# Attention 1 of a four-layer kernel with its scores computed turned: the probabilities come out transposed, the maxima ride along as two rows of the operand

## Reference

```python
q = Wq @ x + bq                       # 256 x 256 by 256 x 1024, for each batch b of 8
k, v = (Wk @ ctx + bk) @ proj_k, (Wv @ ctx + bv) @ proj_v      # 256 x 64, computed earlier
q, k, v = (t.reshape(b, HD, H, -1) for t in (q, k, v))         # HD = 16, H = 16 heads
scores = jnp.einsum('bdhn,bdhk->bhnk', q, k) / HD ** 0.5       # 1024 queries x 64 keys a head
prob = jax.nn.softmax(scores, axis=-1)
out = Wm @ einsum('bhnk,bdhk->bdhn', prob, v) + bm
x = x + tanh(gate) * out              # x is normalised before it; after it come its row statistics
```

## Time and profile before

| | us |
|---|---|
| three runs, median | 1507.66 (1507.24 to 1511.41) |
| the profiled execution | 1511.91 |
| its span, first to last instruction | 1510.2 |
| attention 1 in it | 1085 to 1425 |
| busy over the span: PE / DVE / ACT / POOL | 1381.5 / 974.5 / 747.1 / 427.6 |

### The profile page before, as it was taken

The page is one execution under the profiler, slowest core; times in us unless marked ns, Lnnn a source line. Parts: engine busy times, 40 slices in busy tenths (PEclk is TensorE's granted clock), DMA queues, the critical chain, the costliest instruction groups (busy, mean ns, idle before and its releaser), DMA issues. The chain is left out here.

```text
span 1510.2 us, 28515 instructions
## 1 busy us (share of the span) xinstructions
PE 1381.5 (91%) x10774; PEld 1123.1 (74%) x10782; DVE 974.5 (65%) x1564; ACT 747.1 (49%) x1881; POOL 427.6 (28%) x473
## 2 busy tenths in 40 slices
PE   6998799999999999987999999979779999999388
PEld 6997788979889898855888888868556666666244
DVE  4363277767767767664233256648657999998487
ACT  4231167766767767762111111013157777777286
POOL 0010001101011010111011113223468888887224
PEclk9999889999999999999999999989899999999789
DMA  6743454552544526555534551102332222221023
GB/s 224 240 154 93 81 134 116 141 138 71 147 116 127 151 71 176 140 168 184 186 130 172 195 223 57 42 24 74 109 101 64 64 64 63 63 63 43 1 84 140
DMA packets 127910, 174.93 MB, mean 116 GB/s; under 512 B 27799, under 2 KB 96919, under 8 KB 127792
## 3 DMA queue, kind: packets, MB, share of 16 engines
q1 hardware_dynamic: 127792, 173.26, 39.4%
HBM read 86.94 MB, written 35.29 MB: 81 GB/s over the span
## 5 line engine op out<-in xcount | busy, mean ns | idle before, releaser
L1148 ACT ACTIVATE a_prob<-a_psS,a_negmax 128x256 f32<-128x256 f32 x512 | 237.2, 484 | 159.2 <-DVE a_negmax L1063 159.2
L1063 DVE TENSOR_REDUCE a_negmax<-a_psS 128x4 f32<-128x1024 f32 x128 | 154.1, 1204 | 68.5 <-PE a_psS L956 66.8
L881 POOL COPY a_recip<-a_recip_head 128x256 f32<-128x256 f32 x64 | 25.7, 402 | 528.6 <-DVE a_recip_head L1113 528.6
L931 PE MATMUL a_psQ<-a_xT_hi,wide 128*128 128x256 f32 x912 | 171.1, 288 | 0.4
L1366 PE MATMUL m_psY<-w_ffn,m_a_hi 128*128 128x512 f32 x512 | 160.3, 395 | 9.3 <-DVE m_a_lo L1422 9.3
L1366 PE MATMUL m_psY<-wide,m_a_hi 128*128 128x512 f32 x512 | 159.3, 392 | 6.8 <-DVE m_a_lo L1414 6.8
L966 PE MATMUL a_psT<-ident,a_prob 128*128 128x128 f32 x1024 | 138.6, 280 | 14.3 <-ACT a_probT L1165 5.8
L931 PEld LDWEIGHTS a_psQ<-a_xT_hi,wide 128*128 128x128 f32 x912 | 138.8, 189 | 9.1 <-issue 6.0
L966 PEld LDWEIGHTS a_psT<-ident,a_prob 128*128 128x128 f32 x1024 | 117.4, 144 | 23.6 <-issue 12.6
L1165 ACT COPY a_probT<-a_psT 128x512 f32<-128x512 f32 x208 | 116.0, 610 | 37.6 <-PE a_psT L966 36.5
L931 PE MATMUL a_psQ<-a_xT_lo,wide 128*128 128x256 f32 x456 | 127.5, 280 | 0.0
(11 more groups left out here) (233 smaller groups left out, 3017.7 us busy)
## 6 DMA issues: line engine op xcount, KB each, us to landing
a_q_stack<-a_q_hi SPq DMA_DIRECT2D x128, 128.0 KB, 2.6
a_q_stack<-a_q_lo SPq DMA_DIRECT2D x128, 128.0 KB, 2.6
c_raw<-lay_ctxT SPq DMA_DIRECT2D x16, 512.0 KB, 4.8
rows<-in_x SPq DMA_DIRECT2D x8, 1024.0 KB, 6.6
scratch_o<-a_oT SPq DMA_DIRECT2D x16, 512.0 KB, 3.0
m_x<-in_x SPq DMA_DIRECT2D x8, 1024.0 KB, 5.9
scratch_x<-m_x SPq DMA_DIRECT2D x8, 1024.0 KB, 5.1
b_q_stack<-b_q_hi SPq DMA_DIRECT2D x64, 128.0 KB, 2.3
```

Of the source, the lines that this page charges most:

```text
L881: nc.gpsimd.tensor_copy(recip[:, t % 2], recip_head[:, t % 2].unsqueeze(3).broadcast_to([P, TT, JH0, HD0])).then_inc(recip_ready, 1)
L931: last = nc.tensor.matmul(bank[:, 0:S], w[:, kt, t * P:(t + 1) * P], a[:, kt, :], start=(kt == 0 and w is wq.hi and a is xT_hi), stop=(kt ...
L1063: nc.vector.tensor_reduce(negmax[:, n % 2, :], psS[:, bank:bank + 2, :].rearrange("p a (j k) -> p (a j) k", k=S), AX_X, ALU.max, negate=Tr ...
L1148: last = nc.scalar.activation(prob[:, n % 2, j, :], psS[:, 2 * (n % 2) + j // 2, (j % 2) * S:(j % 2 + 1) * S], ACT.Exp, bias=negmax[:, n % ...
```

## The change

The unit becomes a tile of 128 channels (`t`, eight heads as four pairs `j`) by 512 queries (`h`), four a batch. The work is a list of steps `(b, k)`, k from 0 to 3 and b from -1 to 8, and each engine's program follows it.

- `scores` now makes only approximate scores (high parts alone, one bank `psS` of 128 queries x 8 heads x 64 keys) so that DVE can take negated maxima (`negmax`). It waits for the maximum before it, since there is one bank.
- `turn_shift` transposes the maxima of half a batch, ACT copies them (`copy_shift`), and `stack_shift` puts them by DMA into rows 96 and 97 of `q_stack`.
- `turned_scores` takes keys (`kT`, 98 rows: high, high and low parts, and two rows of ones) as the stationary operand and `q_stack` as the moving one. Its product is the exact score minus the maximum, keys in the partitions. ACT takes the exponential straight into `probT`. Nothing is transposed.
- `values` makes the products with V for 512 queries, and then the sums, with 0/1 matrices (`sum_of`) into `psM`. DVE takes reciprocals of 128 x 256, split into high and low parts, and `spread_reciprocals` spreads them by matmuls with a 0/1 matrix.
- `stack_query` needs three parts (high, low, high) for each of four pairs of heads: 12 DMAs of 32 rows a tile. `load_rows` repeats the keys three times (6 DMAs), and `load_keys`, `load_v1` take one DMA each; `stack_shift` takes 4 DMAs, twice a batch.
- Wq, Wm and the tables are laid out by the host. The ffn weight is loaded at the start of `ffn1_stage`.

```diff
-                for g in range(2):
-                    rows = slice(g * HALF_P, (g + 1) * HALF_P)
-                    for src, half in ((q_hi, g), (q_lo, 1 - g)):
-                        sp.dma_start(plain(q_stack)[half * HALF_P:(half + 1) * HALF_P, t, g, cols],
-                                     plain(src)[rows, m % 2, :]).then_inc(q_stacked[m], 16)
+                if a:
+                    sp.wait_ge(psP_full, 4 * TILES * (a - 1) + PJ * (k + 1))
+                sp.wait_ge(q_lo_ready, TILES * a + k + 1)
+                for part, src in enumerate((q_hi, q_lo, q_hi)):
+                    for j in range(PJ):
+                        sp.dma_start(plain(q_stack)[part * 2 * HD1:(part + 1) * 2 * HD1, t * PJ + j, cols],
+                                     plain(src)[j * 2 * HD1:(j + 1) * 2 * HD1, k % 2, :]).then_inc(q_stacked[k], 16)
+            def stack_shift(a, h):
+                if a:
+                    sp.wait_ge(psP_full, 4 * TILES * (a - 1) + 2 * PJ * (h + 1))
+                sp.wait_ge(shift_ready, 2 * a + h + 1)
+                for t in range(CT1):
+                    for e in range(2):
+                        lo = t * HT1 + e * PJ
+                        sp.dma_start(plain(q_stack)[STACKED + e:STACKED + e + 1, t * PJ:(t + 1) * PJ, h * HALF_N:(h + 1) * HALF_N],
+                                     plain(shift)[lo:lo + PJ, h, :]).then_inc(shift_stacked[h], 16)
 ...
+            for b, k in STEPS:                                   # SP
+                if k == 0 and real(b + 1):
+                    load_rows(b + 1)
+                    load_v1(b + 1)
+                if k == 1 and real(b + 2):
+                    load_keys(b + 2)
+                sa, sk = scored_tile(b, k)                       # (b + 1, k - 1) if k else (b, 3)
+                if real(sa):
+                    stack_query(sa, sk)
+                if k == 1 and real(b):
+                    stack_shift(b, 1)
+                if k == 3 and real(b + 1):
+                    stack_shift(b + 1, 0)
 ...
+            def scores(a, k, i):                                 # PE, four to a tile
+                if n:
+                    pe.wait_ge(max_ready, n)
+                nc.tensor.matmul(psS[:, :], q_hi[:, k % 2, i * P:(i + 1) * P], kbd[:, a % 2, t, :, :].rearrange("p h k -> p (h k)"),
+                                 start=True, stop=True).then_inc(scores_full, 1)
+            def turned_scores(b, k, j):                          # PE, four to a tile
+                if j == 0:
+                    pe.wait_ge(q_stacked[k], QDMAS * (b + 1))
+                    pe.wait_ge(shift_stacked[h], 64 * (b + 1))
+                if n >= 2:
+                    pe.wait_ge(exp_done, n - 1)
+                nc.tensor.matmul(psP[:, n % 2, :], kT[0:ROWS, b % 2, t * PJ + j, :, :].rearrange("p e k -> p (e k)"),
+                                 q_stack[0:ROWS, t * PJ + j, h * HALF_N:(h + 1) * HALF_N], start=True, stop=True
+                                 ).then_inc(psP_full, 1)
```

More of the change, by code:

```diff
@@ L1613, in attn1_stage, with tile_of, output_of @@
     ident = sh.ident
[L1614 to L1632, removed]
+    PAIRS1, STACKED, TILES = NH1 // 2, 3 * 2 * HD1, 4
+    ROWS = STACKED + 2
+    PJ = PAIRS1 // CT1
+    PARTS = 3
+    QDMAS = 16 * PARTS * PJ
+    def tile_of(k):
+        return k % CT1, k // CT1
+    def output_of(b, k):
+        return (b, 0, 0) if k == 3 else (b - 1, *((1, 0), (0, 1), (1, 1))[k])
     with ExitStack() as es:
@@ L1661, in attn1_stage @@
[L1661 to L1667, removed]
+        q_stack = sb("q_stack", [P, PAIRS1, D], F32R)
+        keys = sb("keys", [P, CT1, NK1])
+        kbd = sb("kbd", [P, 2, CT1, HT1, NK1], F32R)
+        krep = sb("krep", [P, PAIRS1, NK1])
@@ L1685, in attn1_stage @@
[L1685 to L1692, removed]
@@ L1697, in _, with real, scored_tile @@
+        block = es.enter_context(nc.Block())
+        STEPS = [(b, k) for b in range(-1, B + 1) for k in range(TILES)]
+        def real(b):
+            return 0 <= b < B
+        def scored_tile(b, k):
+            return (b + 1, k - 1) if k else (b, TILES - 1)
         @block.sync
         def _(sp):
[L1699 to L1703, removed]
-                    for g in range(2):
[L1705 to L1709, removed]
@@ new lines, in spread_reciprocals @@
+            def spread_reciprocals(b, h, t):
+                n = 2 * b + h
+                if t == 0:
+                    pe.wait_ge(recip_low, n + 1)
+                    pe.wait_ge(shift_ready, min(n + 2, 2 * B))
+                else:
+                    pe.wait_ge(o_ready, 2 * n + 1)
+                for part in range(2):
+                    nc.tensor.matmul(psB[:, part * S:(part + 1) * S], spread[:, t, part, :], recip_hi[:, :], start=True, stop=False)
+                    last = nc.tensor.matmul(psB[:, part * S:(part + 1) * S], spread[:, t, part, :], recip_lo[:, :],
+                                            start=False, stop=True)
+                last.then_inc(psB_full, 1)
@@ new lines, in output @@
+            def output(n, b, t, h, dt):
+                if dt == 0:
+                    if n == 0:
+                        pe.wait_ge(wm_loaded, 16)
+                    else:
+                        pe.wait_ge(y_ready, n)
+                    pe.wait_ge(o_ready, 4 * b + 2 * h + 2)
+                last = nc.tensor.matmul(psY[:, :], wmT[:, dt, t * P:(t + 1) * P], o[:, dt, h * HALF_N:(h + 1) * HALF_N],
+                                        start=(dt == 0), stop=(dt == CT1 - 1))
+                if dt == CT1 - 1:
+                    last.then_inc(out_full, 1)
```

759 lines of the change are left out of this document (368 added, 391 removed).

## The result

The changed kernel takes 1547.29 us in the median of 4 executions (1544.73 to 1553.73), the kernel before 1507.52 us (4 executions). The ratio is 1.0264, 95% interval 1.0229 to 1.0300: 39.8 us slower, where 47.4 were forecast (1555 us, range 1510 to 1582). Attention 1, from its first DMA to the end of its last row maximum, grew from 339.9 us (1084.85 to 1424.72, for the end) to 373.0 us (1084.94 to 1457.96). Another 3.7 us lie at the head of the last stage.

A forecast was written before the change was run, and what follows sets the result against it. TensorE bound the kernel before, DVE right behind; afterwards SP's DMA issuing was to bound attention 1. A later start, batches of 42.4 us and a longer end gave +47.4 us: 1555 us, range 1510 to 1582.

The forecast's parts named there:

- SP sets the batch: Attention 1: SP issues 64 DMAs a batch at 0.64 us, 41.0 us, more than PE's 37.8; main case, chance 0.52.
- T = 42.4: Length of an attention 1 batch: 19.4 us to step (b+1, 0), then 36 DMAs, 23.0 us, to step (b+1, 2).
- The wait and the half clock in T: PE idles 3 to 5 us before step (b, 2), then starts at half clock; without the clock's part T is 41.
- First turned score 1126.6: Attention 1, step (0, 0): first stack DMA at 1098, then 41 DMAs (26.2 us) and landing.
- the sum: Attention 1 from start through batches to last row maximum at 1472.1 against 1424.7: +47.4 us.
- The weight load costs nothing under 14 us: Last stage's head: ffn weight needs 8.6 us, first transposes came 14 us after the stage began, so moving it is free.
- PE's terms: TensorE in attention 1: value records and sum records run in waves of four, 1.0 us each, 2.0 together.
- The worse rival: Value records overlap in pairs only, or issues cost more: batch 45 to 48.6 us, 1573 to 1597 us; chance 0.13.
- DVE's terms: DVE in attention 1: reciprocal 2.1 us (lower bound 0.5), low parts 0.4, in all 30 us a batch.
- The first rival: DVE and PE in lockstep, SP not the bound (issue 0.50): 37.8 us a batch, 1528 us; chance 0.22.
- The faster rival: PE sets the pace, issue 0.50 or less, reciprocal near 0.5: 1496 us, needing batches under 35.3 us; chance 0.13.

The follow-up runs named there:

- e2: Changed kernel plus four more DMAs a batch on SP, into a tile nobody reads: 1567.42 us, ratio 1.0386.
- e11: e9 with the x3 work in steps 1 and 3 and the last stage's weight loaded behind GpSimd's reduction: 1509.95 us, ratio 1.0024.
- e5: Changed kernel with 4 of each query tile's 12 DMAs left out from the second batch on: 1534.78 us, ratio 1.0198.
- e7: Changed kernel with query tiles sent through DRAM, five larger DMAs a tile in place of twelve: 1525.77 us, ratio 1.0109.
- e9: e7 with DVE making the low keys behind its x3 work in step k = 1, not ahead of it: 1515.70 us, ratio 1.0054.
- e12: e11 with no early wait for the spreading table, first maxima sent before the third query tile, weight loaded in the last full batch: 1506.65 us, ratio 1.0002.
- e1: Changed kernel with the maxima's 8 DMAs a batch issued by ACT instead of SP: 1545.02 us, ratio 1.0246.
- e13: e12 with GpSimd instead of DVE normalising x2 and making the reciprocals' low parts: 1509.55 us, ratio 1.0026.

## Why the prediction was right, and by which steps

- *SP sets the batch, 41.0 us by 64 issues of 0.64.* Right, and shown by e2. The query tiles cost 0.63 and the maxima 0.65, as taken from the earlier trace rows. The keys' rows cost 0.47, the figure that the earlier trace rows had for 32 rows from DRAM and that the prediction used only as a bound; for v and the keys it was 0.43 and 0.58.
- *T = 42.4.* The term that was mis-sized. From step (0, 0), 1124.54, to step (7, 0), 1410.87, it is 40.9 a batch. The half from step (b, 2) to (b+1, 0) was forecast as 19.4; it is 19.06 in the batch shown (1270.74 to 1289.80) and 18.9 in the mean of seven. The other half, 36 DMAs, was forecast as 23.0 and is 22.0, by the cheaper DRAM reads (8 of the 36). Seven batches make 10.5 us of the error.
- *The wait and the half clock in T.* Right in part. The 28 issues between the maxima of the two halves need 17.8 us by themselves, and two of the seven halves took just that; the others took 19.0 to 19.8, so waits do come on top. PE's seven waits before step (b, 2) were 5.31, 3.89, 3.27, 2.31, 3.19, 2.81 and 1.91 us. Behind the first three and the sixth the granted clock fell to half for 3 to 7 us, and those four halves took 19.4 us in the mean, the forecast; behind the other three it stayed full, and they took 18.2. So the clock's part was there in four batches of seven, and the prediction had it in all. That it lengthened those halves is read from seven cases and not tested.
- *First turned score 1126.6, step (7, 2) 13 to 14 us behind (7, 0), the end 34.4 us later.* Measured 1124.54, 13.6 us (1410.87 to 1424.48), and 33.5 us (to 1457.96). In all the stage grew by 33.1 us where the sum had 47.4. That the ratio's 39.8 us lies nearer is luck in part: 3.7 us are the weight load, which the sum did not have, and about 4 us are the spread of executions, since the profiled one of before was a slow one.
- *The weight load costs nothing under 14 us.* Wrong, 3.7 us. The load itself took about 8.7 us, but it stretched the time before GpSimd's reduction from 5.9 to 9.5 us (e11). The prediction asked when the weight was needed, and not what its transfer delays. The Trainium skill ("GPSIMD Engine Reference", section "Instruction dispatch") says that the first call of a freshly loaded GpSimd kernel pays about 6 us for loading its code; the 5.88 and 5.84 us here agree. That the time before the reduction is code being loaded, and that this is what the 2 MB transfer slowed, is inferred from the page and e11's edit, not seen.
- *PE's terms.* Values and sums cost 34.1 + 33.5 = 67.6 us for 32 tiles, 2.1 a tile: waves of four, 2.0 forecast. The worse rival falls with it, and with issues of 0.63 and maxima of 0.65 each, not 0.76 and 0.85.
- *DVE's terms.* The reciprocal takes 1.75 us (2.1 forecast, within 0.5 to 2.1). The low part takes 1.07 on average (0.4 forecast). The sum, 30 us a batch, was right (29.5 and 31.7).
- *The first rival, lockstep at 37.8 us a batch.* This is the step that failed, unseen while SP was in front: e5 and e7 measure 40 us. Its sum of work was right and its order was not read: `low_keys` stands in DVE's list where it waits 3.3 us for ACT, and 2.0 us of x3 work lies behind it. With that put right (e9) the batch is 37.7, the 37.8 of the prediction. That it agrees so closely is chance, since e11 has 36.6 with the same work in yet another order. That the rival's 1528 us and e7's 1525.77 agree is luck. e7's batches are 1.6 us longer than 37.8, 11 us in seven. But the rival counted the eighth batch in full and then 21.9 us, 59.7 us from step (7, 0) to the end; that batch has no query for a next one, the prediction's main sum had 48.7 us there, and e7 measures 47.2.
- *The faster rival* was to need a batch under 35.3 us. That bound has the same eighth batch in it and is too strict. The best versions here have 36.2 to 36.6 us, with SP, DVE's order, the start and the weight all put right, against 37.7 of before, and the first turned score comes 28.6 us after the stage's first DMA (e12: 1082.15 to 1110.71), against 20.5 us for the first scores of before. In its profile e12's attention 1 takes 336.6 us, 3.3 less than the 339.9 of before, but the ratio over all executions (1.0002) shows no gain; the one profile of before is of a slow execution, so how much of the 3.3 us is the kernel's stays open.

The stage in parts, in us, from the one profile of each run:

| | first DMA to step (0, 0) | a batch, mean from step (0, 0) to (7, 0) | step (7, 0) to the last row maximum | attention 1 |
|---|---|---|---|---|
| forecast | 41.8 | 42.4 | 48.7 | 387.3 |
| changed kernel | 39.6 | 40.9 | 47.1 | 373.0 |
| e1 | 30.9 | 41.3 | 51.8 | 371.8 |
| e5 | 39.8 | 39.7 | 47.2 | 364.8 |
| e7 | 35.2 | 39.4 | 47.2 | 358.4 |
| e9 | 35.8 | 37.4 | 48.3 | 345.8 |
| e11 | 34.7 | 36.7 | 49.4 | 341.1 |
| e12 | 28.6 | 36.8 | 50.8 | 336.6 |
| e13 | 26.7 | 37.3 | 51.7 | 339.6 |

Where the 39.8 us went, by the ratios of the runs in order: issues on SP, with the earlier start that they allow, 23 us (e7), DVE's order 8 (e9), x3's place and the weight load 5 (e11), start and weight 3 (e12). The first is good to about 6 us, the others to 3 or 4.

Left open: a second bank for the scores was not tried, since the changed kernel's eight PSUM banks are all in use. Between e5 and e7 the ratios differ by 0.9%; in the profiles attention 1 differs by 6.4 us, 4.7 of them at the start.

## What to carry to other kernels

Count the DMAs that one queue must issue per stage, times the interval within a series, beside the busy time of the engines: here the queue was the bound at 88 GB/s. When one bound is removed and little comes back, look for the second one in the order of an engine's list, above all at an instruction that waits for another engine with the next stage's input queued behind it. Moving an issue to another engine moves its cost there (four held ACT for 2.61 us). A fix that brings little back need not be a bad one: about half of what e1 fell short by was the second bound and not its edit.

## What the runs showed of the hardware

- The time to issue a DMA did not follow its size. Within SBUF: 0.65 us for 8 KB and 0.63 for 64 KB. From DRAM: 0.42 to 0.47 for 32, 128 and 256 KB. To DRAM: 0.34 to 0.43 for 256 KB. On ACT's queue it cost the same 0.65 (2.61 / 4) and held the engine. The Trainium skill ("DMA: Bandwidth & Descriptors", section "Issuing engines are not separate DMA queues") says that several issuing engines save only the time on the sequencer, usually small relative to the DMA; here it was the bound of a stage.
- A GpSimd instruction holds up one of DVE. The same subtraction of 128 x 256 in the timelines of e11, with no GpSimd instruction beside it, and of e7, with one:

```profile
1306.44 0.43 DVE L1992 TENSOR_TENSOR b_recip_lo<-b_recip,b_recip_hi 128x256 fp32r<-128x256 f32 x1
```

```profile
1317.25 1.36 DVE L1992 TENSOR_TENSOR b_recip_lo<-b_recip,b_recip_hi 128x256 fp32r<-128x256 f32 x1 [0.67 <-ACT b_recip_hi L2106]
1317.07 1.27 POOL L1783 TENSOR_TENSOR b_q_lo<-b_q,b_q_hi 128x512 fp32r<-128x512 f32 x1 [2.27 <-ACT b_q_hi L2088]
```

In e7 GpSimd ends at 1318.34, after its usual 1.27 us, and DVE 0.27 us later. It is the rule in this run: in each of the 12 cases in e7 in which this subtraction overlaps a GpSimd instruction it takes 0.70 to 1.36 us and ends 0.28 us behind it, and in the other 4 it takes 0.42 or 0.43. The Trainium skill ("SBUF — State Buffer", section "SBUF: two separate sides") tells of a port pair that the two lock for a whole instruction; the rows agree.
- How long PE had waited did not alone tell what the clock did. In the changed kernel the granted clock stayed full behind waits of 2.31 and 3.19 us and fell to half behind 2.81 and 3.27; in e7 it fell behind each of five waits of 2.60 us. What half clock costs: the two products of 512 columns took 1.91 us in place of 1.02.
